# Three whole-matrix sums of |w|, moved from a TensorE matmul to GpSimd's partition_all_reduce, in a fused decoder layer on one core

## The reference, cut to what matters

```python
def weight_quant(w):
    wf = w.astype(jnp.float32)
    s = 1.0 / jnp.clip(jnp.mean(jnp.abs(wf)), EPS, None)
    return (jnp.clip(jnp.round(wf * s), -1.0, 1.0) / s).astype(w.dtype)
...
h = jax.nn.silu(bit_linear(x, w_gate)) * bit_linear(x, w_up)
h = rms_norm(h, ln_weight)
return bit_linear(h, w_down)
```

## Time and profile before

| | us |
|---|---|
| median of 3 runs | 984.36 |
| lowest and highest | 982.83, 987.35 |
| the profiled execution, its own time | 982.83 |
| its span in the profile | 981.5 |
| PE busy | 880.1 (90%) |
| DVE busy | 817.0 (83%) |
| ACT busy | 712.5 (73%) |
| POOL busy | 428.2 (44%) |

### The profile page before, as it was taken

How to read it: one execution, slowest core, us unless ns; L and a number is a source line. 1 busy time by engine, 2 the same in 40 slices (tenths; PEclk the granted TensorE clock), 3 DMA queues, 4 the chain that set the end, 5 groups by cost and what they waited for, 6 DMA issues and landing times.

```text
span 981.5 us, 22541 instructions
## 1 busy us (share of the span) xinstructions
PE 880.1 (90%) x8575; PEld 546.3 (56%) x8674; DVE 817.0 (83%) x1520; ACT 712.5 (73%) x1188; POOL 428.2 (44%) x507
## 2 busy tenths in 40 slices
PE   6998878888898989898989899999999998987897
PEld 3456565655565656564556555556565555653453
DVE  4677688997889898998989898989797989897953
ACT  1147384667779797978788788888888878796665
POOL 2110203454454546353636463736364544545532
PEclk9999999999999999999999999999999999999999
DMA  9996360102313333323251616243333333222033
GB/s 359 393 403 224 127 224 13 61 23 62 107 45 94 87 95 86 90 87 89 78 104 65 116 65 115 68 99 82 84 63 101 74 92 79 88 75 73 14 65 97
DMA packets 119388, 107.21 MB, mean 109 GB/s; under 512 B 91792, under 2 KB 94720, under 8 KB 118128
## 3 DMA queue, kind: packets, MB, share of 16 engines
q1 hardware_dynamic: 116320, 100.64, 35.6%
q10 hardware_dynamic: 2336, 2.52, 0.8%
q0 software_dynamic: 624, 2.59, 0.7%
HBM read 65.62 MB, written 10.75 MB: 78 GB/s over the span
## 4 chain that ended last, share of the span: by engine, by line
PE 38%; DVE 20%; ACT 17%; issue 10%; DMA 5%; POOL 5%; SPq 2%; DVEq 0%; ACTq 0%; POOLq 0%
PE bank L653 10%; PE bank L673 8%; PE bank L590 7%; PE bank L582 4%; ACT arena L957 3%; DVE fs L1535 2%; ACT junk L1022 2%; PE bank L563 2%; ACT work L996 2%; PE bank L613 2%; DVE rows L1436 2%; DVE amax L1504 2%; DVE stats_wkv L1492 2%; ACT junk L1027 1%; DVE junk L1526 1%
## 5 line engine op out<-in xcount | busy, mean ns | idle before, releaser
L1858 POOL TENSOR_TENSOR work<-junk,lnw 128x512 f32<-128x512 f32 x128 | 175.2, 1387 | 182.7 <-DVE junk L1526 182.2
L653 PE MATMUL bank<-w_up_gate,qT 128*128 128x512 bf16 x967 | 227.0, 381 | 18.2 <-DMA qT<-q_tok 6.8
L653 PEld LDWEIGHTS bank<-w_up_gate,qT 128*128 128x128 bf16 x1024 | 95.2, 98 | 126.5 <-DMA qT<-q_tok 9.0
L957 ACT ACTIVATE arena<-bank 128x384 f32<-128x384 f32 x256 | 104.8, 497 | 32.6 <-PE bank L582 32.5
L673 PE MATMUL bank<-w_down,work 128*128 128x512 bf16 x470 | 112.1, 381 | 17.2 <-ACT junk L1022 6.7
L1027 ACT ACTIVATE junk<-junk,deq 128x512 f32<-128x512 f32 x128 | 92.6, 723 | 41.7 <-DVE junk L1526 41.3
L1526 DVE TENSOR_TENSOR junk<-bank,junk 128x512 f32<-128x512 f32 x128 | 85.0, 680 | 41.7 <-issue 25.0
L563 PE MATMUL bank<-wide,wq_sb 128*128 128x256 f32 x512 | 116.1, 385 | 1.3 <-DVE rows L1436 1.3
L613 PE MATMUL bank<-wo_sb,wide 128*128 128x512 f32 x256 | 113.9, 597 | 1.5 <-DVE wide L1429 1.5
L996 ACT ACTIVATE work<-work,fs 128x2048 f32<-128x2048 f32 x32 | 64.0, 2001 | 67.6 <-DVE fs L1548 67.6
L563 PEld LDWEIGHTS bank<-wide,wq_sb 128*128 128x128 f32 x512 | 97.2, 192 | 24.9 <-issue 11.8
(11 more groups left out here) (156 smaller groups left out, 1550.2 us busy)
## 6 DMA issues: line engine op xcount, KB each, us to landing
sums<-in_xT SPq DMA_DIRECT2D x8, 1024.0 KB, 9.8
wide<-in_xT SPq DMA_DIRECT2D x16, 512.0 KB, 4.6
wide<-wide SPq DMA_DIRECT2D x64, 128.0 KB, 2.1
out<-rows SPq DMA_DIRECT2D x32, 256.0 KB, 2.1
rows<-in_x SPq DMA_DIRECT2D x15, 512.0 KB, 3.6
ctx_T<-in_ctxT SPq DMA_DIRECT2D x15, 512.0 KB, 4.5
kv_b<-k_raw SPq DMA_DIRECT2D x64, 96.0 KB, 2.2
work<-in_wgT SPq DMA_DIRECT2D x4, 1024.0 KB, 13.9
```

The costliest lines, as they stand in the source:

```text
L653: last = te.matmul(bank[4 + k % 4][:, :], qT[:, c, t * P:(t + 1) * P], w_up_gate[:, m, c, cols], start=c == 0, stop=c == NC - 1)
L957: se.activation(prob[:, :, QUAD * c + j, :], bank[j][:, 0:NW * P].rearrange("p (k q) -> p k q", k=NW), ACT.Sigmoid, scale=float(1.0 / np.s ...
L1858: ge.tensor_tensor(hid_w[:, t, cols], hid[:, n % 2, :], lnw[:, cols], op=ALU.mult).then_inc(z_set.sem, 1)
```

## The change

`weight_total(m)` leaves PE's program and enters POOL's. The order of sums is turned round: DVE first adds the four columns of `abs_sums` in SBUF (now L1351, it waits for ACT's `w_summed`), POOL then runs `partition_all_reduce` with add on the 128 x 1 column (L1824, it waits for DVE's `w_col`), and DVE takes the mean from its output `abs_tot`. The ones column and its memset go, and so does PE's wait for `w_col[DOWN]` in `gate_up`, which had guarded bank 5.

```diff
         def weight_mean(m):
+            ve.wait_ge(w_summed[m].sem, w_summed[m].at(0))
+            ve.tensor_reduce(abs_sum[:, m:m + 1], abs_sums[:, m, :], AX.X, ALU.add).then_inc(w_col[m].sem, 1)
             ve.wait_ge(w_all[m].sem, w_all[m].at(0))
-            ve.tensor_reduce(abs_sum[:, m:m + 1], bank[5][:, m * NC:(m + 1) * NC], AX.X, ALU.add).then_inc(w_col[m].sem, 1)
-            ve.wait_ge(w_col[m].sem, w_col[m].at(0))
-            ve.tensor_scalar(w_mean[:, m:m + 1], abs_sum[:, m:m + 1], 1.0 / (I * D), QUANT_EPS, ALU.mult,
+            ve.tensor_scalar(w_mean[:, m:m + 1], abs_tot[:, m:m + 1], 1.0 / (I * D), QUANT_EPS, ALU.mult,
                              ALU.max).then_inc(w_mean_set[m].sem, 1)
...
-        def weight_total(m):
-            te.wait_ge(w_summed[m].sem, w_summed[m].at(0))
-            te.matmul(bank[5][:, m * NC:(m + 1) * NC], one_col[:, :].to_broadcast([P, P]), abs_sums[:, m, :], start=True,
-                      stop=True, skip_group_check=True).then_inc(w_all[m].sem, 1)
...
+        def weight_total(m):
+            ge.wait_ge(w_col[m].sem, w_col[m].at(0))
+            ge.partition_all_reduce(abs_tot[:, m:m + 1], abs_sum[:, m:m + 1], P, bass.bass_isa.ReduceOp.add).then_inc(
+                w_all[m].sem, 1)
...
-                if k == 1 and f == 0:
-                    te.wait_ge(w_col[DOWN].sem, w_col[DOWN].at(0))
...
         ext_total()
+        weight_total(GATE)
         load_lnw()
         weigh_windows(0, 0)
         weigh_windows(0, 1)
         weigh_windows(0, 2)
         weigh_windows(0, 3)
+        weight_total(UP)
         att_rstd(0)
         key_steps(0)
         first_state(0)
+        weight_total(DOWN)
         outputs(0, 0)
```

More of the change, by code:

```diff
@@ L66, in build @@
     abs_sum = sb("abs_sum", [P, 3])
-    one_col = sb("one_col", [P, 1])
+    abs_tot = sb("abs_tot", [P, 3])
     w_mean = sb("w_mean", [P, 3])
@@ L207, in build @@
     out_stored = [event(f"out_stored{t}", unit=16) for t in range(NT)]
-    eps_set, win_set = event("eps_set", 7), event("win_set", 4)
+    eps_set, win_set = event("eps_set", 6), event("win_set", 4)
     key_bn, key_mv = event("key_bn", 2 * NT), event("key_mv", 2 * NT)
@@ L706, in tensor_program @@
         spin(0, 0, 5)
-        weight_total(GATE)
         scores(0, 0)
@@ L725, in tensor_program @@
         attention_out(0, 0)
-        weight_total(UP)
         attention_out(0, 1)
@@ L737, in tensor_program @@
         scores(1, 3)
-        weight_total(DOWN)
         dens(1, 0)
@@ L1269, in constants @@
             ve.memset(per_row[:, :], 1.0 / I).then_inc(eps_set.sem, 1)
-            ve.memset(one_col[:, :], 1.0).then_inc(eps_set.sem, 1)
         def first_den():
```

## The result

The changed kernel takes 994.89 us (median of 4 runs, 992.13 to 996.42) against 984.84 us for the kernel before beside it (median of 4). The medians lie 10.1 us apart. The ratio on record is 1.0083 with a 95% interval of 1.0063 to 1.0103, which is 8.2 us; it is worked out from all the runs and is not the quotient of the two medians. The forecast was 987.5 with a range from 982.5 to 993: slower was right in direction, which had got a chance of 0.38, and the time lies beyond the range.

A forecast was written before the change was run, and what follows sets the result against it. No single engine was taken as the bound; the chain passes the UP sum and POOL behind DOWN. UP's 0.74 and DOWN's 2.42 gave 3.2 us, added to the median 984.36 for 987.5, range 982.5 to 993.

The forecast's parts named there:

- The bound and the two places: Between 70 and 160 us no engine bounds alone; the chain is touched at the UP sum and behind the DOWN sum.
- UP: Sum at the output projection: DVE waits for POOL's switch, 0.74 us late with S of 5.6, breaking even at 4.86.
- DOWN: Sum near 143 us: way in covered; POOL's switch back makes the second multiply S - 3.18 late, 2.42 us.
- GATE: Sum near 79 us: no switch needed; DVE loses about 0.5 us, swallowed by later idle time, so nought.
- The idle time before the first window: DVE's idle time before 95.6 us should shrink from 2.5 to 2.0, with nothing moved there.
- S: How long POOL is away after a code switch: between 1.28 and 9.85 us, taken as 5.6.
- The ceiling of 8.3: Upper bound on S in us, from POOL's switch pair at 1.0 being over by 9.31, if it loads anything.
- The clock: Longer PE waits at 112 or 156 may earn another dip to 1.2 GHz, costing up to 1.7 us.
- Rival 2: Long switch: from S = 4.9 each microsecond costs two, at UP and behind DOWN; 992.9 us at 8.3; chance 0.33.
- Rival 1: Short switch, S under 4: UP gains more than DOWN loses; at 3.2 and below -1.8 us, 982.5; chance 0.12.
- Rival 3: Switch paid at the first call, so no waiting covers it: about 18 us, 1002; chance 0.05.
- a delay at 157 is kept to the end: Lateness from POOL's second multiply reaches PE's transposes at 156.63 and counts whole, as nothing in that chain waits for outside things.

The follow-up runs named there:

- the control: Kernel before with PE's own short waits filled: 2 spin matmuls before row 1's queries, 6 instead of 3 before the WKV output's transposes; 1.0000 of before.
- the covered switches: Kernel before plus three all-reduces on POOL that nobody waits for, six code switches more, placed where POOL is idle; 987.63 us, 1.0015 of before.
- GATE alone: Against the kernel before, only the GATE sum goes to POOL, UP and DOWN stay on PE; 985.98 us, 0.9992 of before.

## Why the prediction was wrong, point by point

- **The bound and the two places** were right. The losses stand at UP on DVE and behind DOWN on POOL, where the prediction put them. GATE was nought (0.9992), also as worked out. The idle time before the first window did not shrink to 2.0 as said (it is 2.58), because in this profile DVE reached its passes 0.8 us earlier, more than the 0.54 us for which it had waited for POOL.
- **The step that failed is the size of S.** I took 5.6 us, the middle between ACT's table load of 1.28 and the looser ceiling of 9.85, and one value for both directions. The runs show 5.8 to 6.8 us into the reduce's code and 6.9 to 8.1 back, from the end of the pair, where it stands free of other waits. With 6.5 and 7.7 in the prediction's own formulas, UP is 6.5 - 4.86 = 1.6 and DOWN 7.7 - 3.18 = 4.5, in all 6.2 us instead of 3.2. The middle was not sound: the table load is another engine's and had no claim to be the lower end. The ceiling of 8.3 held at both places, but not for every switch: 8.7 us directly behind the DMA issue.
- **UP** was measured at 1.9 us of lateness in the profile; the formula with 6.5 gives 1.6. Most of the rest is that the pair ended 0.24 us behind the fourth window, where I had counted 0.04.
- **DOWN**: the first multiply came 4.6 us after ACT was done with its input (146.88), where before it came 0.15 after it (145.15 + 0.63, against 145.93). So it was 4.45 us late, as the formula says (7.7 - 2.7 = 5.0, less the 0.55 us by which ACT was itself later against the DOWN sum). The second multiply was 3.4 us late in its distance to ACT, not 4.5: the same 0.55 is gone, and another 0.5, since the multiply behind the switch took 1.17 us where it had taken 1.63. DVE was idle beside it, where before it ran a pass of its own; that this is the reason was not tested.
- **The clock was named, priced at up to 1.7 us, and left out of the sum.** That was the second failure. Keeping PE busy through the waits gave back 2.4 to 4.1 us, and the control nothing; so the longer waits cost some 3 us more than their own length. The matmuls show it too: in the three profiles of the changed kernel the transposes and the second projection took 2.5 to 3.1 us longer than before (1.06 and 7.03). The price of 1.7 held for one stretch of 3.4 us; the changed kernel had two of 6.8 in its first profile and one in each of the two others.
- **The sum, mended.** The formulas with the measured switches and the 3.3 us of the clock give 9.5, where 6.5 to 8.2 were measured: the formulas are too high. Distances within the profiles say where the loss stands. From the all-reduce of `ext_total` to the second multiply, the three profiles of the changed kernel take 87.7 to 88.4 us, and five with neither UP nor DOWN on POOL 82.7 to 84.4 (the sixth, with the covered switches and its late load, 85.9); that is some 4.5 us, and not 6.2. From there to the end of the span they take 832.2 to 835.8 against 829.6 to 834.0, some 3 us in the mean, where the low clock behind DOWN stands. The 4.5 also agrees with what was left with both waits filled, 2.9 and 4.1. Of the missing 1.7 us, the item on DOWN names 1.1; the rest lies before it and is open.
- **Rival 2** is what happened, by its mechanism at both places, with the clock on top. Its weight of 0.33 was too low. The range left the clock out; with its ceiling of 992.9 and the clock's price of 1.7 it would have gone to 994.6, and the first median, 994.89, would still have been just beyond.
- **Rival 1** has fallen: no switch in any run was under 5.7 us.
- **Rival 3** has fallen: the DOWN reduce started 0.14 us after DVE's column was there (143.20 to 143.34), 20 us behind its switch, and the load had cost nothing at the call. The Trainium skill, "GPSIMD Engine Reference", section 2.1 Instruction dispatch, gives about 6 us (5.95) between the switch and the first instruction, less any wait. For the way in the runs agree, 5.8 to 6.8. For the way back they show more, 6.9 to 8.1, and the measurement decides. Its figure in the prediction's sum would have given 3.9 us, still half of the loss.
- **That a delay at 157 is kept to the end** holds by the times, within their noise: 7.7 us of adds on POOL, by the formula some 4 us of lateness at the second multiply, cost 4.3 us of the whole.

## What to carry to other kernels

An operation of GpSimd that lives in another piece of code than its neighbours costs two switches, here about 6.3 us in and 7.6 back, and the idle time that hides them must lie on each side of it separately: the DOWN sum had 20 us ahead of it and only 2.7 behind. Look in POOL's queue, not at the busy time of the operation (0.4 us), and put such an operation next to another of the same code, as the GATE sum was, where it is free. When a new wait makes TensorE idle for several microseconds, count more than its length: here spins through two such waits gave back about 3 of the 7 us lost, though no data came earlier.

## What the runs showed of the hardware that I had not expected

- The two directions differ: 5.8 to 6.8 us into the code of the all-reduce (eleven cases), 6.9 to 8.1 us back to that of the elementwise operations (nine cases; 8.7 in the one directly behind a DMA issue). What sets the length within these ranges is open. Nothing but two records of under 0.1 us shows it; the idle time carries the word "issue".
- The all-reduce itself is cheap: 0.40 us on 128 x 1 and 0.39 on 128 x 4 (0.62 and 0.96 in two of the three that nobody waited for), and DVE goes on 0.44 us after its start.
- Dips of PE's clock do not stay where they are. The changed kernel had low stretches at 113, 143 and 160 in one profile, and at 147 and 164 in another. The kernel before and GATE alone, alike there for PE, had 3.4 and 10.2 us at the lower level from about 141 on. The place where the profiles agree best is the second projection, as said above.
